# The opening of layer 1: biases in one transfer, separate banks, constant products in TensorE's waits, later statistics

## The reference, cut to what matters

```
x = x + LN(attn1(LN(x)))      # x: (16, 256, 128), 16 heads of 8 channels, float32
x = x + LN(block2(LN(x)))     # 4-head attention over the batch axis, then 8 experts

attn1: qkv = x @ w_qkv.T + b_qkv;  q, k, v = split(qkv)
       attn = softmax(q k.T / sqrt(128)) per head;  heads = attn @ v
       return heads @ w_o.T + b_o + x
```

## Time and profile before

| | us |
|---|---|
| median of three runs | 626.78 (620.87 to 627.47) |
| profiled execution, first to last instruction | 624.8 |
| first score product of layer 1 | starts at 23.5 |
| iteration 0 | 46.2 to 67.4 |
| a later iteration of layer 1 | 16.93 |
| last of layer 1's x, added by GpSimd | 333.3 |
| TensorE busy, of the span | 84% |
| VectorE, ScalarE, GpSimd busy | 72%, 57%, 50% |

### The profile page before, as it was taken

The page is one execution under the profiler, slowest core; times in us unless marked ns, Lnnn a source line. Parts: engine busy times, 40 slices in busy tenths (PEclk is TensorE's granted clock), DMA queues, the critical chain, the costliest instruction groups (busy, mean ns, idle before and its releaser), DMA issues. The chain is left out here.

```text
span 624.8 us, 15886 instructions
## 1 busy us (share of the span) xinstructions
PE 524.8 (84%) x5168; PEld 383.2 (61%) x5168; DVE 448.6 (72%) x1274; ACT 358.2 (57%) x969; POOL 314.3 (50%) x523
## 2 busy tenths in 40 slices
PE   2899999999999999999972899999957249999910
PEld 2576666666666565666641677677736249999910
DVE  2255878888888888888842789998685626888860
ACT  1214567676676656677560688876653025767760
POOL 5140244433445567422133638887884610477776
PEclk9999999999999988999995899997775559999965
DMA  4300523111011100101111000000001122244333
GB/s 98 87 2 2 170 71 38 24 23 20 19 20 19 21 19 3 20 19 20 20 36 34 35 2 2 2 3 10 20 31 38 59 77 68 34 60 64 32 33 31
DMA packets 38099, 21.62 MB, mean 35 GB/s; under 512 B 13433, under 2 KB 36353, under 8 KB 38018
## 3 DMA queue, kind: packets, MB, share of 16 engines
q1 hardware_dynamic: 18544, 10.65, 7.6%
q0 software_dynamic: 6640, 4.92, 5.6%
q10 hardware_dynamic: 12834, 5.04, 3.2%
HBM read 10.11 MB, written 8.12 MB: 29 GB/s over the span
## 5 line engine op out<-in xcount | busy, mean ns | idle before, releaser
L331 DVE TENSOR_REDUCE nmax<-psA 128x2 f32<-128x512 f32 x256 | 164.9, 685 | 63.7 <-PE psA L209 63.1
L493 ACT ACTIVATE pr<-psB 128x512 f32<-128x512 f32 x250 | 136.0, 595 | 95.1 <-PE psB L226 94.9
L209 PE MATMUL psA<-km,qp 24*128 24x256 f32 x768 | 128.9, 432 | 2.2 <-DVE nmax L331 1.7
L226 PE MATMUL psB<-q,km 26*128 26x256 f32 (+1 forms) x752 | 112.6, 416 | 0.2 <-DMA q<-mT 0.2
L209 PEld LDWEIGHTS psA<-km,qp 24*128 24x128 f32 x768 | 81.2, 200 | 34.8 <-DVE nmax L331 22.6
L1627 POOL DMA_INDIRECT out<-wz,ys x39 | 63.3, 1624 | 53.0 <-ACT wz L1582 44.1
L586 POOL TENSOR_TENSOR km<-kraw,rows_of 128x768 f32<-128x768 f32 x16 | 23.5, 1467 | 122.7 <-ACT kraw L468 115.1
L226 PEld LDWEIGHTS psB<-q,km 26*128 26x128 f32 (+1 forms) x752 | 70.0, 191 | 1.3 <-DMA q<-mT 0.6
L240 PE MATMUL psO<-pr,v 128*32 128x256 f32 x1024 | 70.3, 393 | 0.1
L1180 ACT ACTIVATE prob<-psS,nbias 128x128 f32<-128x128 f32 x128 | 45.6, 386 | 7.0 <-DVE nbias L998 7.0
L240 PEld LDWEIGHTS psO<-pr,v 128*32 128x32 f32 x1024 | 27.2, 111 | 33.8 <-issue 22.5
(11 more groups left out here) (201 smaller groups left out, 1113.5 us busy)
## 6 DMA issues: line engine op xcount, KB each, us to landing
q<-mT SPq DMA_DIRECT2D x256, 1.0 KB
ys<-y_sorted SPq DMA_DIRECT2D x39, 72.0 KB, 1.9
e_w<-W ACTq DMA_DIRECT2D x1, 2048.0 KB
e_w<-W ACTq DMA_DIRECT2D x4, 512.0 KB
xs<-x_all SPq DMA_DIRECT2D x16, 128.0 KB
out<-x_all SPq DMA_DIRECT2D x15, 128.0 KB, 3.8
x_all<-x SPq DMA_DIRECT2D x1, 1536.0 KB, 8.9
out<-wz,ys POOLq DMA_INDIRECT x39, 3.3
```

What stands on the lines that cost most here:

```text
L209: last = T.matmul(psA[:, (16 * b + n) % 3, c * L1:(c + 1) * L1], query_part(b, h, depth, c), keys(b, h, depth, slice(0, L1)), start=True, ...
L226: last = T.matmul(bank_of(b, h)[:, c * L1:(c + 1) * L1], keys(b, h, depth, slice(c * P, (c + 1) * P)), queries(b, h, depth, slice(0, L1)), ...
L331: V.tensor_reduce(nmax[:, b % 2, hf, :, at], psA[:, (16 * b + n) % 3, :].rearrange("p (c m) -> p c m", c=2), AX.X, ALU.max, negate=True).t ...
L493: A.activation(pr[:, h % PRING, :, :].rearrange("p c l -> p (c l)"), bank_of(b, h), ACT.Exp, scale=SCALE1).then_inc(S["b_free"], 1)
```

## The change

- The biases come in one DMA to a row `braw`, second in SyncE's queue; five small copies on ScalarE spread them. `w_o` comes in one DMA to `w_nat`, and a copy on ScalarE rearranges it.
- The products of element 0 have banks of their own (`psA`, `psB`), counted by `first_pe`, `first_act` and `first_dve`. Queries and keys of element 0 are made in one run, keys first. VectorE makes `km` of element 0 straight from PSUM (three instructions) and `qp` (two), ScalarE half of the weights' copies.
- `keep_warm(n)` issues n products of a constant 128 x 128 by 128 x 512 in bfloat16 into `psO`, which is not read: 8, 3, 2 and 7 of them in the opening, and 2 behind each of n = 9, 11 and 13.
- An `Exp` of one column on ScalarE comes ahead of all its other work.
- Statistics: EARLY = 4. Those of element 1 come behind `qp` of element 0, those of 3 behind n = 7; those of 4 to 15 in iterations 0 to 11. GpSimd's `norm_x(1)` comes behind the memsets of `v32`.

The core of the diff:

```
@@ -19,7 +19,10 @@
 
 HALF = 8
 SLOTS = 4
-EARLY = 8
+EARLY = 4
+FIRST_W, FIRST_BIAS, FIRST_X, FIRST_K, FIRST_Q, FIRST_V = range(1, 7)
+WO_TURNED, BIAS_ROWS, FIRST_XT = 1, 6, 7
+WARM, BIAS_COLS = 1, 2
 LAST = B1 - 1
 PRING = 8
 
...
-            pe.wait_ge(S["ld_w"], 16)
-            pe.wait_ge(S["ld_wo"], 64)
-            for k in range(4):
-                last = T.transpose(misc[:, k * P:(k + 1) * P], w_nat[:, k, :], ident[:, :])
-            last.then_inc(S["full"], 1)
-            begin("bias")
-            pe.wait_ge(S["brow0"], 4)
-            pe.wait_ge(S["ld_b"], 192)
-            for k in range(2):
-                for t in range(2):
-                    last = T.matmul(misc[:, 2 * k + t:2 * k + t + 1], brow[0:1, k, t, :], one[:, :],
-                                    start=True, stop=True)
-            last = T.matmul(misc[:, 4:5], bv_row[0:1, :], one[:, :], start=True, stop=True)
-            last.then_inc(S["full"], 1)
+            def keep_warm(n):
+
+                for _ in range(n):
+                    T.matmul(psO[:, :], warm[:, 0:P], warm[:, :], start=True, stop=True)
 
             def prep_x(b):
                 begin("xT", b)
...
+            keep_warm(8)
+            pe.wait_ge(S["consts"], 2)
+            pe.wait_ge(S["ld_w"], 32)
+            T.transpose(psA[:, 2, 0:P], w_nat[:, 0, :], ident[:, :]).then_inc(S["first_pe"], 1)
+            for k in (1, 2):
+                T.transpose(misc[:, k * P:(k + 1) * P], w_nat[:, k, :], ident[:, :])
+            pe.wait_ge(S["first_act"], WO_TURNED)
+            T.transpose(misc[:, 3 * P:4 * P], wo_nat[:, :], ident[:, :]).then_inc(S["full"], 1)
+
+            pe.wait_ge(S["brow0"], 4)
+            pe.wait_ge(S["first_act"], BIAS_ROWS)
             for k in range(2):
                 for t in range(2):
-                    prep_qk(0, k, t)
-            prep_v(0)
+                    T.matmul(psB[:, 1, 2 * k + t:2 * k + t + 1], brow[0:1, k, t, :], one[:, :],
+                             start=True, stop=True)
+            T.matmul(psB[:, 1, 4:5], bv_row[0:1, :], one[:, :], start=True, stop=True).then_inc(S["first_pe"], 1)
+            keep_warm(3)
+            pe.wait_ge(S["xn_ok"], 1)
+            for c in range(2):
+                last = T.transpose(psB[:, 0, c * P:(c + 1) * P], xn[:, 0, c, :], ident[:, :])
+            last.then_inc(S["first_pe"], 1)
+            keep_warm(2)
+            pe.wait_ge(S["w_ok"], 5)
+            pe.wait_ge(S["first_act"], FIRST_XT)
+            for k in (1, 0):
+                for t in range(2):
+                    last = T.matmul(psA[:, 1 - k, t * L1:(t + 1) * L1], wqk[:, k, t, :], xnT[:, 0, :], start=True,
+                                    stop=True)
+                last.then_inc(S["first_pe"], 1)
+            for c in range(2):
+                last = T.matmul(psB[:, 2, c * P:(c + 1) * P], xnT[:, 0, c * P:(c + 1) * P], wvo[:, 0, :],
+                                start=True, stop=True)
+            last.then_inc(S["first_pe"], 1)
+            keep_warm(7)
             for n in range(16):
                 scores_for_max(0, n)
                 if n == 1:
@@ -288,6 +311,9 @@
                     prep_qk(1, n // 2 - 1, 1)
                 if n == 7:
                     prep_v(1)
+                if n in (9, 11, 13):
+                    keep_warm(2)
+            pe.wait_ge(S["v_ok"], 1)
             for i in range(LAST + 2):
                 iteration(i)
 
...
-
+            V.memset(warm[:, :], 1.0).then_inc(S["first_dve"], 1)
             dve.wait_ge(S["consts"], 2)
             V.tensor_reduce(same32[:, :], ident[:, :].rearrange("p (g r) -> p r g", r=32), AX.X,
...
...
+            V.tensor_copy(wqk[:, 1, 0, :].rearrange("p (g r) -> p g r", r=32)[:, :, 0:24]
+                          .rearrange("p g (i c) -> p i g c", c=C1),
+                          misc[:, P:P + 96].rearrange("p (i g c) -> p i g c", g=4, c=C1)).then_inc(S["w_ok"], 1)
+            V.tensor_copy(wqk[:, 1, 1, :].rearrange("p (g r) -> p g r", r=32)[:, :, 0:C1],
+                          misc[:, P + 96:2 * P].rearrange("p (g c) -> p g c", c=C1)).then_inc(S["w_ok"], 1)
+            V.tensor_copy(wvo[:, :, :].rearrange("p a d -> p (a d)"), misc[:, 2 * P:4 * P]).then_inc(S["w_ok"], 1)
+            dve.wait_ge(S["w_ok"], 5)
+            dve.sem_inc(S["free"])
+            dve.wait_ge(S["first_pe"], FIRST_BIAS)
+            V.tensor_copy(b_cols[:, :], psB[:, 1, 0:5]).then_inc(S["first_dve"], 1)
+            dve.wait_ge(S["first_dve"], BIAS_COLS)
+            dve.wait_ge(S["m_step"], 3)
+            dve.wait_ge(S["first_pe"], FIRST_K)
+            for i in range(3):
+                last = V.tensor_scalar(km[:, 0, i, :], psA[:, 0, 0:L1], b_cols[:, 2:3], rows_of[:, i:i + 1], ALU.add,
+                                       ALU.mult)
+            last.then_inc(S["km_ok"], 1)
+            dve.wait_ge(S["q_ok"], 2)
+            for t in range(2):
+                V.tensor_copy(qp[:, 0, t, :].rearrange("p (c k r) -> p k c r", c=2, r=32),
+                              q[:, 0, t, :].rearrange("p (k c r) -> p k c r", c=2, r=32)).then_inc(S["q_ok"], 1)
+            stats_x(1)
             stats_x(2)
-            between = {1: 3, 3: 4, 7: 5, 9: 6, 11: 7}
             dve.wait_ge(S["w_zero"], 2)
+            between = {7: 3}
             for n in range(16):
                 maxima(0, n)
                 if n % HALF == HALF - 1:
@@ -436,7 +469,9 @@
                 act.wait_ge(S["full"], turns[name] + 1)
 
             def turned_x(b):
-                if b >= 2:
+                if b == 2:
+                    act.wait_ge(S["first_pe"], FIRST_V)
+                if b > 2:
                     ready("v", b - 2)
                 ready("xT", b)
...
-            for a in range(4):
-                act.dma_start(w_nat[:, 3, :].rearrange("p (j a c) -> p a j c", a=4, c=C1)[:, a, :, :],
-                              w_o.rearrange("p (a j c) -> p a j c", j=4, c=C1)[:, a, :, :]).then_inc(S["ld_wo"], 16)
-            act.wait_ge(S["free"], 2)
-            for b in range(2):
-                turned_x(b)
-                queries_in(b)
-                keys_in(b)
-                queries_in_parts(b)
-                if b == 0:
-                    act.wait_ge(S["v_zero"], 2)
-                values_in(b)
+            act.dma_start(w_nat[:, 3, :], w_o).then_inc(S["ld_w"], 16)
+            act.wait_ge(S["first_dve"], WARM)
+            A.activation(primed[:, :], warm[:, 0:1], ACT.Exp)
+            act.wait_ge(S["ld_w"], 32)
+            A.activation(wo_nat[:, :].rearrange("p (j a c) -> p j a c", a=4, c=C1),
+                         w_nat[:, 3, :].rearrange("p (a j c) -> p j a c", j=4, c=C1), ACT.Copy).then_inc(S["first_act"], 1)
+            act.wait_ge(S["brow0"], 4)
+            act.wait_ge(S["ld_b"], 16)
+            for k in range(2):
+                whole = braw[:, k * P:(k + 1) * P].rearrange("o (i g c) -> o i g c", g=4, c=C1)
+                to = brow[:, k, :, :].rearrange("o t (g r) -> o t g r", r=32)
+                A.activation(to[:, 0, :, 0:24].rearrange("o g (i c) -> o i g c", c=C1), whole[:, 0:3, :, :],
+                             ACT.Copy).then_inc(S["first_act"], 1)
+                A.activation(to[:, 1, :, 0:C1], whole[:, 3, :, :], ACT.Copy).then_inc(S["first_act"], 1)
+            A.activation(bv_row[:, :].rearrange("o (j a c) -> o a j c", a=4, c=C1),
+                         braw[:, 2 * P:3 * P].rearrange("o (a j c) -> o a j c", j=4, c=C1),
+                         ACT.Copy).then_inc(S["first_act"], 1)
+            act.wait_ge(S["w_zero"], 1)
+            act.wait_ge(S["first_pe"], FIRST_W)
+            A.activation(wqk[:, 0, 0, :].rearrange("p (g r) -> p g r", r=32)[:, :, 0:24]
+                         .rearrange("p g (i c) -> p i g c", c=C1),
+                         psA[:, 2, 0:96].rearrange("p (i g c) -> p i g c", g=4, c=C1),
+                         ACT.Copy).then_inc(S["w_ok"], 1)
+            A.activation(wqk[:, 0, 1, :].rearrange("p (g r) -> p g r", r=32)[:, :, 0:C1],
+                         psA[:, 2, 96:P].rearrange("p (g c) -> p g c", c=C1), ACT.Copy).then_inc(S["w_ok"], 1)
+            act.wait_ge(S["first_pe"], FIRST_X)
+            A.activation(xnT[:, 0, :], psB[:, 0, 0:L1], ACT.Copy).then_inc(S["first_act"], 1)
+            act.wait_ge(S["first_dve"], BIAS_COLS)
+            act.wait_ge(S["first_pe"], FIRST_Q)
+            for t in range(2):
+                A.activation(q[:, 0, t, :], psA[:, 1, t * L1:(t + 1) * L1], ACT.Identity,
+                             bias=b_cols[:, t:t + 1]).then_inc(S["q_ok"], 1)
+            act.wait_ge(S["km_ok"], 1)
+            for t in (1, 0):
+                A.activation(kraw[:, 0, t, :], psA[:, 0, t * L1:(t + 1) * L1], ACT.Identity,
+                             bias=b_cols[:, 2 + t:3 + t]).then_inc(S["k_ok"], 1)
+            act.wait_ge(S["first_pe"], FIRST_V)
+            act.wait_ge(S["v_zero"], 2)
```

(61 more changed lines are left out.)

24 lines of the change are left out of this document (2 added, 22 removed).

## The result

The changed kernel takes 620.71 us (median of 16 runs, 614.82 to 626.94) against 626.73 for the kernel before (16 runs, 620.87 to 629.04). The ratio is 0.9898, interval 0.9873 to 0.9924, so 6 us less. Ratios and their intervals leave out executions that are over 1.5% above the fastest of the same kernel. Two further comparisons, on two more chips, gave 0.9851 (0.9809 to 0.9894) and 0.9892 (0.9841 to 0.9943). The forecast was 620.8.

What follows compares the result with a forecast made beforehand. It took a long opening, a chain of single waits run at TensorE's lower clock level, as the bound. Terms -7.5 + 0.8 + 0.7 gave -6.0, so 618.8 for the profiled execution and 620.8 for the median; range 607 to 629.

Steps and rivals of the forecast that it cites:

- The start: Opening up to the first score product: it comes at 16.0 instead of 23.54, -7.5 us, between -3.4 and -9.5.
- The wait for `xn` of element 1: Before element 1's transposes: TensorE waits on statistics now behind `qp`, n = 2 about 3.5 after the first score; +0.8 us.
- The fall of the clock around that wait: Around `prep_x(1)`, near 19 to 20 us: clock falls back, so element 0's maxima run at the lower level as before.
- The late constants: Constant products at three places in element 0's maxima: +1.4, half returned by statistics taken away; +0.7 us (0 to 2.7).
- Iteration 0 at the lower level as before: First 12.35 us of iteration 0 stay at the lower clock level, unchanged, with an error of 3 us either way.
- Moved statistics: Statistics of 12 to 15 moved into iterations 8 to 11: 0 in the sum, 3 us in the range.
- Sum for the opening: Start, wait and late constants together: -7.5 + 0.8 + 0.7 = -6.0 us.
- Rival 1: Clock holds through `prep_x(1)`, so element 0's maxima go at VectorE's pace: -18, 609 us; chance 0.20.
- second and third rival: Second: no clock rise before first score, at 20.1, 624 us, chance 0.15. Third: late rise in iteration 0, 631, chance 0.15.

Runs made afterwards that it cites:

- second kernel that holds it: Changed kernel with element 1's statistics early, four constants behind n = 1, two behind 7 and 9, three behind 11, 13, 15; 602.72 us, ratio 0.9638.

## Why the prediction was right, point by point

- **The start: -7.5 forecast, -11.0 measured**, outside the -3.4 to -9.5 given. The steps were right, two sizes were not: the weights were in at 4.3 instead of 4.7 with ScalarE's bias copies done at 5.4 instead of 6.4, and the clock rose at 5.94, right behind the first burst, so that bias products, projections and constants all ran at the upper level. I had expected it in the projections, had priced an early rise at a first score of 15 (-8.5), and the lower end of -9.5 was worked out from nothing. It does not carry the result: without constants the start is still -9.0.
- **The wait for `xn` of element 1: +0.8 forecast, +0.4 measured** (15.60 - 12.55 = 3.05 against 2.64). The statistics to `xn` took 12.05 to 15.12, the 3.07 that was carried over.
- **The fall of the clock around that wait: right**, at 16.18, 0.9 behind its end (forecast near 19 to 20, from a later start). That the fall comes from what TensorE does there is shown by filling the wait.
- **The late constants: +0.7 forecast, +2.5 measured** (three groups 2.98 apart for 2.14), 3.1 by the run without them. This term was mis-sized: I let 0.4 of each pair hide in an idle time under VectorE and half of the removed statistics come back. The rows show no such overlap: a pair starts at 28.31 as the group before it ends, and the next group at 29.27 as the pair ends. And the statistics had been hidden already, as the run with their old places shows.
- **Iteration 0 at the lower level as before: right**, 12.1 us for 12.35, the rise moved from 58.55 to 50.31. Ahead of the rise stands the first `attend` (at 57.79 before, at 49.69 now); the projection that I named beside it comes at 60.23, behind the rise.
- **Moved statistics: 0 forecast, none measured.** I had read one fall of the clock in iterations 8 and 9 of the kernel before. There are two, at 225.80 and 246.28, and they lie in iterations 10 and 11, which last 20.0 each. The first profile of the change has one, in iteration 10; iteration 11 lasts 18.4, which saves 1.6 us. The second profile has one in iteration 11, the third none: that is the chance of single executions.
- Sum for the opening: -6.0 forecast, -8.1 in the profile (38.20 for 46.30), which is -11.0 + 0.4 + 2.5. In the times it is -6.0, -8.9 and -6.0 in the three comparisons. Two errors of opposite sign stand behind that: the start was 3.5 better than forecast, the constants 1.8 worse. They leave the opening 2.1 better than the forecast, and later falls of the clock win or lose as much again in single executions. That 620.71 lies 0.1 from 620.8 is luck; what was right is the direction, the size to some 3 us, and the fall of the clock.
- **Rival 1** (the clock holds, 609 in all, 12 below the forecast) was wrong for the change and near as a price: in the second kernel that holds it iteration 0 starts 8.9 earlier and the transposes in iteration 1 come 13.7 earlier (50.0 for 63.8); the medians on one chip, 602.72 and 618.30, are 15.6 apart. That kernel also has its statistics early.
- The Trainium skill's rule that asks only for bursts not far apart ("TensorE: Matmul & The Clock Gate", "Why this matters for your kernels") did not hold here: with 1.57 us of waiting, and in the kernel with the statistics early with TensorE busy for 3.10 of 3.10, the clock fell.
- Of the second and third rival nothing was seen in the three profiles of the change: the clock rises at 5.94, 5.72 and 5.58, and again at 50.31, 50.09 and 49.95.

## What to carry to other kernels

Read TensorE's clock from the length of equal products where the record has not begun. Constant products are worth their time only if the clock they raise is kept until the real work fills the array; a burst ahead of one unfilled wait bought nothing here, and eight more in the wait itself bought about 1% (0.9792, where the change has 0.9851 to 0.9898). When work is moved behind a chain of waits, ask who stands behind it: here 0.8 us of statistics, moved behind the queries, set the start of the next element and with it the clock.

## What was not expected of the hardware

- The clock fell behind stretches in which TensorE was busy for all of 3.10 us and, in another kernel, for all of 3.45, mostly with products of 24 and 8 rows; with four constants among them it held. The time TensorE is busy does not by itself tell whether it holds its clock.
- Behind eight constant bfloat16 products of 512 columns (3.60 us, from 1.51 on) the rise comes at 4.6 to 6.5 in seven of the nine profiles that have them at the start, and in the other two only at 10.9. Of the three profiles of the change without constants in its opening, one has a rise at 12.33, at its projections; in the other two the record begins at 42.2 and 52.0.
- Two executions of the same kernel differ by 5 us in their spans (614.0 and 619.1) with the same opening, by a fall of 3.4 us in iteration 1 and other places of the falls later.
